# Row fetches in all groups of the last layer of a graph network, and the tile's arithmetic on VectorE

## The reference

```python
def gnn(x, src, dst, type, W_rel, W_root, bias):            # x: layernorm of the input
    for l in range(3):
        xr = einsum('nd,rde->rne', x, W_rel[l])
        agg = segment_sum(xr[type, src], dst, 6250)
        x = relu(agg + x @ W_root[l] + bias[l])
    return x

def ffn(x, weight, bias):                                   # x: layernorm of (input + gnn)
    lx, lw = log(abs(x) + 1e-8), log(abs(weight) + 1e-8)
    mx, mw = max(lx, -1), max(lw, -1)
    log_out = log(exp(lx - mx) @ exp(lw - mw).T) + mx + mw.T
    return sign(sign(x) @ sign(weight).T) * exp(log_out) + bias
```

## Time and profile before

| | us |
|---|---|
| median of 3 runs | 5843.94 (5837.36 to 5844.55) |
| the profiled execution | 5849.7 |
| its span | 5847.9 |

### The profile page before, as it was taken

How to read it: one execution, slowest core, us unless ns; L and a number is a source line. 1 busy time by engine, 2 the same in 40 slices (tenths; PEclk the granted TensorE clock), 3 DMA queues, 4 the chain that set the end, 5 groups by cost and what they waited for, 6 DMA issues and landing times. The chain is left out here.

```text
span 5847.9 us, 124600 instructions
## 1 busy us (share of the span) xinstructions
PE 4261.5 (73%) x26004; PEld 3871.9 (66%) x26005; DVE 1828.3 (31%) x3531; ACT 622.0 (11%) x848; POOL 4322.0 (74%) x4573
## 2 busy tenths in 40 slices
PE   3777777777777677777777767677777777777776
PEld 2766666766676666666666666667667676667666
DVE  4222222222222222222222222223333334334333
ACT  3010101110110010000000000001111101111111
POOL 4777777777777677777777777767777777777775
PEclk9999999899899898999999999988888888888888
DMA  6444444444444343444334334333333333333332
GB/s 193 115 118 116 118 116 117 118 117 117 116 118 117 113 115 112 113 113 113 112 113 113 113 112 114 112 111 114 113 113 114 114 113 114 113 113 114 114 112 83
DMA packets 314263, 674.98 MB, mean 115 GB/s; under 512 B 96052, under 2 KB 168217, under 8 KB 313850
## 3 DMA queue, kind: packets, MB, share of 16 engines
q0 software_dynamic: 218256, 596.28, 35.9%
q1 hardware_dynamic: 54580, 42.39, 2.5%
q10 hardware_dynamic: 41014, 32.79, 1.9%
HBM read 645.39 MB, written 25.68 MB: 115 GB/s over the span
## 5 line engine op out<-in xcount | busy, mean ns | idle before, releaser
L454 POOL DMA_INDIRECT rows<-node_table,idx x4547 | 4314.6, 949 | 1473.4 <-issue 1316.4
L476 PE MATMUL bank<-onehot,rows 128*128 128x128 f32 x18188 | 2665.3, 307 | 1245.1 <-DMA rows<-node_table,idx 518.2
L476 PEld LDWEIGHTS bank<-onehot,rows 128*128 128x128 f32 x18188 | 2513.2, 219 | 1391.9 <-issue 1376.5
L551 PE MATMUL bank<-wrel,agg 128*128 128x256 f32 x5568 | 1282.2, 390 | 23.7 <-DVE agg L1156 23.6
L1133 DVE TENSOR_TENSOR agg<-bank,agg 128x256 f32 x1563 | 662.6, 424 | 1964.4 <-PE bank L476 1432.8
L551 PEld LDWEIGHTS bank<-wrel,agg 128*128 128x128 f32 x5568 | 1082.6, 197 | 177.4 <-issue 27.6
L1034 DVE TENSOR_TENSOR onehot<-bank,key 128x1152 f32<-128x1152 f32 x525 | 707.7, 1348 | 0.9 <-DVEq L1143 0.6
L1165 DVE SCALAR_TENSOR_TENSOR acc<-bank,in_first,acc 128x256 f32 x174 | 84.2, 484 | 1933.3 <-PE bank L551 1809.4
L800 ACT COPY agg<-zero_col 128x2304 f32 x174 | 367.3, 2111 | 1621.2 <-PE bank L551 1083.3
L876 ACT ACTIVATE new_x<-acc 128x256 f32 (+1 forms) x98 | 40.8, 416 | 1635.0 <-DVE acc L1166 874.9
L825 ACT COPY acc<-bank 128x256 f32 (+1 forms) x98 | 36.5, 373 | 1142.9 <-issue 987.0
(11 more groups left out here) (140 smaller groups left out, 903.0 us busy)
## 6 DMA issues: line engine op xcount, KB each, us to landing
far_rows<-node_table SPq DMA_DIRECT2D x12020, 1.0 KB
far_rows<-node_table ACTq DMA_DIRECT2D x6156, 1.0 KB
rows<-node_table,idx POOLq DMA_INDIRECT x4547
node_table<-new_x ACTq DMA_DIRECT2D x98, 128.0 KB
x_tile<-node_table SPq DMA_DIRECT2D x58, 128.0 KB
x_in<-in_x_dram SPq DMA_DIRECT2D x8, 768.0 KB, 11.3
wrel<-in_L_gnn_W_rel_dram SPq DMA_DIRECT2D x6, 1024.0 KB, 8.1
xres<-in_x_dram ACTq DMA_DIRECT2D x48, 128.0 KB
```

Of the source, the lines that this page charges most:

```text
L454: pool.indirect_dma_start(rows[:, s:s + D], None, tables[layer % 2], bass.IndirectOffsetOnAxis(ap=idx[:, g * TPG + k, j:j + 1], axis=0),). ...
L476: last = nc.tensor.matmul(to[:, h, :], row, hot[:, hot_k * CH + j, :], start=(j == 0), stop=(j == CH - 1))
L551: last = nc.tensor.matmul(out_ps, agg[:, half * KH + h, r, 0:P], wrel[:, h, r * D:(r + 1) * D], start=(r == 0 and h == 0), stop=(r == R - ...
```

## The change

- Layer 2 fetches the last 128 rows of every group as layers 0 and 1 do: SP 74 rows, ACT 54, POOL 26 gathers. SP's loop, the counts that TensorE waits for (`far_landed`), and the copy for groups that span too many tiles (`extra_tiles`) lose their separate case.
- In layer 2 ACT does in a group: 22 rows of the next group; if the group is late, the square root, the load of the next tile of the input, and the store of the result of the tile before; then 32 rows. It clears nothing, copies nothing, and makes no signs.
- VectorE in layer 2 clears the half of `agg` behind add k=4 of every group (2304 elements a partition). In a late group it makes the signs of z in two passes ahead of the magnitudes, copies the turned tile behind k=5, and makes the sign of the signs' product in two passes ahead of the result.
- In layers 0 and 1 ACT issues its 54 rows at one go; its copy of the next sums, between the two parts before, comes behind both.

```diff
@@ SP
-            def fetch(layer, g, b, q, rows=SP_ROWS):
+            def fetch(layer, g, b, q):
...
-                        if layer < L - 1:
-                            multiplied(layer, g)
-                            for q in range(QUARTERS - 1):
-                                fetch(layer, g, m % 2, q)
-                        elif m % 2:
-                            multiplied(layer, g)
-                            for q in range(QUARTERS):
-                                fetch(layer, g, 1, q, P)
+                        multiplied(layer, g)
+                        for q in range(QUARTERS - 1):
+                            fetch(layer, g, m % 2, q)
@@ POOL
-                        for j in range(CH - 1 if k == TPG - 1 and (layer < L - 1 or g % 2) else CH):
+                        for j in range(CH - 1 if k == TPG - 1 else CH):
@@ ACT
+            def multiplied(layer, g):
                 if not isinstance(g, int):
                     act.wait_ge(agg_added, g * TPG + (layer * TRIPLES + 3 - TPG))
                     act.sem_inc(act_mark, 1)
...
+            def fetch_rows(layer, g, b, between=None):
+                multiplied(layer, g)
+                fetch_part(layer, g, b, QUARTERS - 2, SP_ROWS % LOADS)
+                if between:
+                    between()
+                fetch_part(layer, g, b, QUARTERS - 1, 0)
...
             def group(layer, g, late=None):
                 gg = g + layer * GROUPS
+                if layer == L - 1:
+
+                    def between():
+                        with act.If(g < late[0]):
+                            ended(layer, late[1])
+                            out_of_tile_before(late[1])
+
+                    fetch_ahead(layer, g, between if late else None)
+                    return
...
-                if layer < L - 1:
-                    fetch_ahead(layer, g, fetch_first)
+                fetch_ahead(layer, g)
                 if late:
                     with act.If(g < late[0]):
-                        if layer < L - 1:
-                            next_sums(layer, late[1])
-                        else:
-                            turned_tile(late[1])
-                            out_of_tile(late[1])
-                if layer < L - 1:
-                    fetch_ahead(layer, g, fetch_second)
+                        next_sums(layer, late[1])
...
-                act.wait_ge(z_ready, t + 1)
-                act.sem_inc(act_mark, 1)
-                nc.scalar.activation(sgn[:, :], z[:, :], ACT.Sign).then_inc(sgn_ready, 1)
-
-            def turned_tile(t):
-
-                act.wait_ge(mag_transposed, t + 1)
-                act.sem_inc(act_mark, 1)
-                nc.scalar.copy(magT[:, :, :], mag_ps).then_inc(magT_ready, 1)
-                nc.scalar.copy(sgnT[:, :, :], sgn_ps).then_inc(sgnT_ready, 1)
-
-            def out_of_tile(t, last=False):
-
-                act.wait_ge(lns_ready, t + 1)
-                act.sem_inc(act_mark, 1)
-                nc.scalar.activation(osgn[:, :], lns_sign_ps, ACT.Sign).then_inc(osgn_ready, 1)
...
+            def out_of_tile_before(t):
+
+                with act.If(t > 0):
+                    before = nc.s_assert_within(t - 1, 0, TILES - 2, skip_runtime_bounds_check_because="the branch is taken behind the first tile")
+                    act.wait_ge(out_done, before + 2)
+                    act.sem_inc(act_mark, 1)
+                    act.dma_start(out[ds(before * P, P), :], res[:, :]).then_inc(out_stored, 16)
@@ VectorE
+                    if layer == L - 1 and k == TPG // 2:
+
+                        nc.vector.tensor_copy(agg[:, ds((g + 1) % 2 * KH, KH), :, :].rearrange("p h r s -> p (h r s)"),
+                                              zero_col[:, :].to_broadcast([P, KH * R * SLOTS])).then_inc(agg_zeroed, 1)
+                    if late and k == TPG // 2 + 1:
+                        with dve.If(g < late[0]):
+                            turned_tile(late[1])
...
-                link(t, 0, nc.vector.scalar_tensor_tensor(mag[:, :], z[:, :], -1.0, z[:, :], ALU.mult, ALU.max))
+                link(t, 0, nc.vector.tensor_single_scalar(sgn[:, :], z[:, :], 0.0, ALU.is_lt))
+                nc.vector.scalar_tensor_tensor(sgn[:, :], z[:, :], 0.0, sgn[:, :], ALU.is_gt, ALU.subtract).then_inc(sgn_ready, 1)
+                link(t, 1, nc.vector.scalar_tensor_tensor(mag[:, :], z[:, :], -1.0, z[:, :], ALU.mult, ALU.max))
...
+            def turned_tile(t):
+                dve.wait_ge(mag_transposed, t + 1)
+                dve.sem_inc(dve_mark, 1)
+                nc.vector.tensor_copy(magT[:, :, :], mag_ps).then_inc(magT_ready, 1)
+                nc.vector.tensor_copy(sgnT[:, :, :], sgn_ps).then_inc(sgnT_ready, 1)
 
             def result(t):
-                dve.wait_ge(osgn_ready, t + 1)
+                dve.wait_ge(lns_ready, t + 1)
                 dve.sem_inc(dve_mark, 1)
-                link(t, 5, nc.vector.scalar_tensor_tensor(z[:, :], lns_ps, mmax[:, 0:1], wmax_bc[:, :], ALU.mult, ALU.mult))
-                link(t, 6, nc.vector.tensor_tensor(z[:, :], z[:, :], osgn[:, :], ALU.mult))
+                link(t, 6, nc.vector.tensor_single_scalar(osgn[:, :], lns_sign_ps, 0.0, ALU.is_lt))
+                link(t, 7, nc.vector.scalar_tensor_tensor(osgn[:, :], lns_sign_ps, 0.0, osgn[:, :], ALU.is_gt, ALU.subtract))
+                link(t, 8, nc.vector.scalar_tensor_tensor(z[:, :], lns_ps, mmax[:, 0:1], wmax_bc[:, :], ALU.mult, ALU.mult))
+                link(t, 9, nc.vector.tensor_tensor(z[:, :], z[:, :], osgn[:, :], ALU.mult))
```

More of the change, by code:

```diff
@@ L361, in multiplied @@
                     sp.sem_inc(sp_mark, 1)
-            def fetch(layer, g, b, q, rows=SP_ROWS):
-                first, end = q * LOADS, min(rows, (q + 1) * LOADS)
+            def fetch(layer, g, b, q):
+                first, end = q * LOADS, min(SP_ROWS, (q + 1) * LOADS)
                 for p, start in zip(range(first, end), far_starts(SP, g, q, 0, end - first)):
-                    sp.dma_start(far_row(p, b), far_from(layer, start)).then_inc(far_by_sp[layer][b][p // (rows // 2)], 16)
+                    sp.dma_start(far_row(p, b), far_from(layer, start)).then_inc(far_by_sp[layer][b][p // SP_HALF], 16)
             def first_layer(g, b, tile):
@@ L388, in _ @@
                 sp.wait_ge(stored, 16 * TILES * layer + 16)
-                if layer < L - 1:
-                    fetch(layer, 0, 0, 0)
+                fetch(layer, 0, 0, 0)
                 load_weights(layer)
-                if layer < L - 1:
-                    for q in range(1, QUARTERS - 1):
-                        fetch(layer, 0, 0, q)
+                for q in range(1, QUARTERS - 1):
+                    fetch(layer, 0, 0, q)
                 with sp.Fori(0, FETCHED // SP_UNROLL) as i:
@@ L479, in far_landed @@
             def far_landed(layer, g, b):
-                if layer < L - 1:
[L481 to L488, removed]
-                        pe.wait_ge(far_by_sp[layer][b][h], g * (8 * HALF) + 8 * HALF)
+                pe.wait_ge(gathered[TPG - 1], g * (16 * (CH - 1)) + (layer * FETCHED + 1) * (16 * (CH - 1)))
+                for h in range(2):
+                    pe.wait_ge(far_by_sp[layer][b][h], g * (8 * SP_HALF) + (2 - b) * 8 * SP_HALF)
+                pe.wait_ge(far_by_act[layer][b], g * (8 * ACT_ROWS) + (2 - b) * 8 * ACT_ROWS)
             def rows_of(layer, g, k, b=None):
@@ L589, in group @@
                             pe.sem_inc(pe_mark, 1)
-                            products(seg[k % 3], rows, onehot[:, k // BATCH, :, :], k, k % BATCH, 0 if layer < L - 1 else None).then_inc(seg_ready, 1)
+                            products(seg[k % 3], rows, onehot[:, k // BATCH, :, :], k, k % BATCH, 0).then_inc(seg_ready, 1)
                         pe.sem_inc(pe_mark, 1)
@@ L770, in _, with fetch_part @@
             act.wait_ge(far_at_ready, 1)
-            def fetch_quarter(layer, g, b, q, first):
-                for m, start in enumerate(far_starts(SCALAR, g, q, first, LOADS)):
+            def fetch_part(layer, g, b, q, first, end=LOADS):
+                for m, start in enumerate(far_starts(SCALAR, g, q, first, end)):
                     act.dma_start(far_row(q * LOADS + first + m, b), far_from(layer, start)).then_inc(far_by_act[layer][b], 16)
-            def fetch_first(layer, g, b):
+            def multiplied(layer, g):
                 if not isinstance(g, int):
@@ L789, in fetch_ahead @@
                     with act.If(g % 2 > 0):
-                        part(layer, ahead, 0)
+                        fetch_rows(layer, ahead, 0, between)
                     with act.Else():
-                        part(layer, ahead, 1)
+                        fetch_rows(layer, ahead, 1, between)
                     act.sem_inc(act_mark, 1)
+                if between:
+                    with act.If(g > FETCHED - 2):
+                        between()
+                        act.sem_inc(act_mark, 1)
             def group(layer, g, late=None):
```

(8 more changed lines are left out.)

49 lines of the change are left out of this document (13 added, 36 removed).

## The result

| | kernel before | changed kernel |
|---|---|---|
| median (4 runs each, same chip) | 5844.24 us | 5973.95 us (5971.58 to 5977.33) |
| ratio, 95% interval | | 1.0226 (1.0213 to 1.0239): slower |
| span of the profiled execution | 5847.9 us | 5975.6 us |
| layer 2, first to last gather | 1927.3 us, 1535 gathers | 2035.8 us, 1506 gathers |
| layer 2, last gather to the end | 45.4 us | 65.3 us |

The spans differ by 127.7 us, and all of it lies in layer 2: its first gather starts at 3874.45, against 3875.25.

The account below looks back on a forecast made before the run. Two near-equal bounds in layer 2: POOL's gathers (33.3 us a group) and the VectorE-TensorE loop (33.9). Tile-ending groups grow 0.8 + 0.25 + 1.5 + 1.2 = 3.75; layer +155, end +5, first group -1: +159, 6002 us, range 5925 to 6070.

Parts of the forecast that it names:

- Two bounds close together, one relieved and one loaded: Layer 2: POOL's 33.3 us a group and the VectorE-TensorE loop's 33.9; the change relieves the first and loads the second.
- Signs of z: On VectorE ahead of the magnitudes in a tile-ending group: all of it on the chain, +0.8 us.
- Clear: On VectorE between add k=4 and k=5: 1.5 us, mostly hidden in a wait; +0.25 us a tile-ending group in mean.
- Copies: VectorE's copies of the transposed tile behind add k=5 delay TensorE's products of k=7 and k=8: +1.5 us.
- Sign of the sum: Two PSUM passes on VectorE ahead of the result in a tile-ending group: +1.2 us.
- The way back: From fold to next group's first add: taken as unchanged when a tile-ending group grows by 3.75 us, to 37.6.
- First groups: Start of layer 2, ahead of the loop's steady state: POOL's fewer gathers save 1 us.
- Row fetches at nothing: SP's and ACT's row fetches in every group of layer 2 cost nothing, having about two groups of time.
- Port: POOL's gathers in layer 2: each VectorE clear delays one by 0.75 to 1.1 us, costing nothing beside the longer loop.
- Rival (a): POOL stays layer 2's bound and pays for gathers delayed by the clear: 5870 us, growth under 0.7 us, chance 0.06.
- rival (b): VectorE's waits in a tile-ending group, 4.8 us, swallow the new work, 4.3 us: 5828 us, chance 0.06.
- (c): Half of the new work in a tile-ending group hides, growth 1.7 us: 5908 us, chance 0.10.

Follow-up runs that it names:

- experiment 1: VectorE's new work alone (clear, signs of z, copies, sign of the sum), fetches as before, against the kernel before: 5968.12 us, ratio 1.021.
- Experiment 3: The clear alone moved to VectorE in layer 2, against the kernel before: 5886.63 us, ratio 1.0076.
- experiment 2: The change's row fetches alone, tile arithmetic and clear left on ACT, against the kernel before: 5938.23 us, ratio 1.0163.
- 6: Changed kernel's fetches; ACT clears and makes signs, VectorE copies, ended tile multiplied behind k=7, result behind the fold; against the kernel before: 5839.48 us, ratio 0.9992.

## Why the prediction was right, step by step

5973.95 us lies in the range, 28 below the forecast of 6002, and the forecast's mechanism is the one that the runs show: 1 has the whole loss without the fetches, in late groups of the forecast's kind. Its terms:

- **Two bounds close together, one relieved and one loaded.** Shown by both sides. Experiment 3 slows POOL alone and costs 0.76%; experiment 1 slows the loop alone and costs 2.1%; the 29 gathers fewer bring nothing in the changed kernel.
- **Signs of z**: 0.8 forecast, 0.76 measured.
- **Clear**: one instruction of 1.35 us, against 1.5 taken and 2.7 as the upper bound. In the chain 0.25 forecast; growth of add k=5 beyond that of k=2 is 1.03 - 0.76 = 0.27.
- **Copies**: 1.5 forecast; 2.30 - 1.03 = 1.27 measured. The bf16 copy takes 0.28 and not 0.40, and TensorE waited 0.9 to 1.0 us for it.
- **Sign of the sum**: 1.2 forecast, 3.45 - 2.30 = 1.15 measured at the fold; the osgn passes start 1.15 ahead of L1196. But it doesn't reach the end of the round everywhere, as the next term shows.
- **The way back**, from the fold to the next first add, is the term that was mis-sized. The step "a late group grows by 0.8 + 0.25 + 1.5 + 1.2 = 3.75" takes it as unchanged, as if TensorE's product with the weights waited for nothing but the fold. The fold did move by 3.45, but the way back became shorter, 13.66 in place of 14.08, so a late group grew by 3.03 only. The reason lies in TensorE's order: the product with the weights also comes behind the first two products of the next group. Where these end later than the fold, a later fold costs less. Group 53 before, then in the changed kernel, and group 16 before for comparison:

```profile
5682.38 4.54 PE L476 MATMUL bank<-onehot,rows 128*128 128x128 f32 x24 [1.93 <-issue]
5684.23 0.42 DVE L1156 TENSOR_TENSOR agg<-agg  x1
5686.77 7.07 PE L551 MATMUL bank<-wrel,agg 128*128 128x256 f32 x32
```

```profile
5796.71 4.54 PE L468 MATMUL bank<-onehot,rows 128*128 128x128 f32 x24 [1.96 <-issue]
5799.68 0.43 DVE L1133 TENSOR_TENSOR agg<-agg  x1
5801.09 7.07 PE L537 MATMUL bank<-wrel,agg 128*128 128x256 f32 x32
```

```profile
4453.91 2.92 PE L476 MATMUL bank<-onehot,rows 128*128 128x128 f32 x24 [1.71 <-DVE agg L1133]
```

In group 53 the two products take 4.54 us in place of 2.92, at a granted clock of 0.60 in the mean against 1.00: the clock stood at its lower level, 1.2 GHz, for most of them, behind 1.93 us of idle time. The product with the weights starts 2.54 us behind the start of the fold before, and 1.41 behind it after, so the 1.15 of the sign of the sum is hidden there.

Of the 47 x 0.42 = 20 us, 15.0 lie in the 13 late groups that had such slow products before. Another 6.9 lie in six groups (8, 9, 10, 12, 14, 46) in which TensorE waited for a gather between the two products before, and in none of them after: its waits for gathers fell from 31 (42.7 us) to 6 (15.6 us) in layer 2, which fits a longer loop that leaves the gathers more time. The other 28 groups together lose 2.1. Why the clock was low in those 13 groups is not shown: the earlier trace rows, group 49, where TensorE idled 1.94 us at the same place, has the products at 2.92. There the way back is 13.67, and growth of the fold, 3.09, and of the period, 3.12, agree. The small remainders of the four terms above, 3.75 - 3.45 = 0.30, are another 14 us: 47 x 3.03 = 142 in place of 176. These 34 us are a little more than the 31 between the forecast's 159 and the 128 measured.

- **Groups without a tile's end**: 28 forecast, 27.7 measured (30.5 before), -22 us.
- **First groups**: -1 forecast. From the layer's first gather to the first add of group 2 it took 94.5 us, against 91.2: +3.3, of the other sign. In group 0 TensorE waits for gathers, up to 4.3 us at a time. The cause is open. The row fetches alone don't do it: experiment 2, which has them too, took 91.4 us for the same stretch, and 6 took 93.8.
- **End**: +5 forecast; from the first add of group 57 to the end 50.3 against 45.3, +5.0.
- **Row fetches at nothing**: right in the changed kernel (no wait for `far_rows`, the square root in time). The order in which ACT works was what made it so: experiment 2 shows the price with the arithmetic left between the rows, and 6 a smaller one with the clear ahead of the root.
- **Port**: 0.75 to 1.1 per clear forecast, absorbed. Experiment 3 measures 0.8 where it isn't absorbed.

The sum: 142 - 22 + 5 + 3.3 - 0.8 = 128 us, the difference of the spans.

Rival (a) asked for growth under 0.7, rival (b) under 0.35; it was 3.03. (a)'s mechanism is real, as 3 shows: POOL pays 46 us for the clears, and in the changed kernel these vanish beside the loop's 108. (b) fell where it was expected to: VectorE's waits at k=5, 7 and 8 did not swallow the work, in group 49 the one ahead of k=7 even grew, from 2.00 to 2.80 us, since TensorE waits for what VectorE now does. The growth also stays above (c)'s 1.7.

**Still open**: what the copies alone and the result behind the fold are worth on a chip where the loop is the bound; and what makes single rows slow to issue on some chips.

## What to carry to other kernels

An engine with 31% busy time can be the bound, when it and a second engine wait for each other in turn: time one round of that loop, and compare it with the busiest engine's time for the same round, before moving work to the "idle" one. Work moved off an engine's queue doesn't come free either way: look at where in the round the new owner does it, and who waits for what comes behind it. Where two bounds lie within a few per cent, expect little from relieving one. And before adding a delay to the round, look at what else the next step waits for: where an engine's own work or a gather ends later than the delayed result, part of the delay is hidden, in the groups where it does so.

## What had not been expected of the hardware

- The same kernel takes 5844 us on some chips and 7996 to 8076 us on others, at a mean granted clock of 0.78 instead of 0.89 to 0.90. 22 single rows need 9.4 to 10.7 us to issue on ACT there (medians of six traces), against 7.4. The same change is then judged differently: VectorE's work costs 2.1% on the one, nothing on the other.
- A copy of 2304 fp32 elements a partition, all read from one zero, took VectorE 1.35 us, and ACT 2.11. On VectorE it holds up a gather of POOL, and how long depends on which starts first: a gather already under way ends 0.12 us behind the copy, one that starts while it runs 0.81 or 0.82 behind it.
